# Taking node tiles by rank of edge count, and running each finished tile's norm, activation and next-layer tables between the gather's steps

## The reference, cut to what matters

```python
for l in range(4):
    h = einsum('ni,rio->rno', X, W[l])               # one table of rows for each of 4 relations
    msg = h[etype, src] * inv_deg[:, None]           # a row for each edge
    agg = segment_sum(msg, dst, num_segments=6250)
    out = agg + X @ root[l] + bias[l]
    out = layer_norm(out) * gamma[l] + beta[l]       # over the 256 features of a node
    X = elu(out) + X
```

## Time and profile before

| what | value |
|---|---|
| median of 3 runs | 8877.58 us (8870.69 to 8877.74) |
| the profiled execution's own time | 8865.25 us |
| its span in the trace | 8863.5 us |
| busy share of the span | PE 71%, PEld 40%, DVE 53%, ACT 15%, POOL 50% |
| granted TensorE clock, mean | 0.792 of full speed |

### The profile page before, as it was taken

One profiled execution on the slowest core, in us unless ns is written; L12 is line 12 of the kernel. 1 busy time (PEld: TensorE's weight loads), 2 busy tenths in 40 slices (PEclk: granted clock), 3 DMA queues, 4 the chain that ended last, 5 costly groups with the idle time before them and its releaser, 6 DMA issues. The chain is left out here.

```text
span 8863.5 us, 101707 instructions
## 1 busy us (share of the span) xinstructions
PE 6322.2 (71%) x18072; PEld 3511.4 (40%) x18072; DVE 4665.9 (53%) x14830; ACT 1360.0 (15%) x3463; POOL 4442.4 (50%) x4395
## 2 busy tenths in 40 slices
PE   0677777587777587777678998818849877774378
PEld 0343333244444244444334333305524444443355
DVE  6135555427777526777633555552243566662522
ACT  0221111231111131111031000002202111110122
POOL 0047777327777516777624777730000477773211
PEclk9988888797777697788687555559869888876789
DMA  2243333234444223333323333300014333330000
GB/s 66 77 136 105 105 105 105 67 106 117 117 117 117 76 91 113 111 112 111 95 73 105 105 105 105 105 24 0 0 45 140 121 105 105 105 105 19 0 24 16
DMA packets 424513, 765.22 MB, mean 86 GB/s; under 512 B 84857, under 2 KB 288845, under 8 KB 424194
## 3 DMA queue, kind: packets, MB, share of 16 engines
q0 software_dynamic: 200240, 547.36, 21.6%
q1 hardware_dynamic: 224206, 217.15, 7.2%
HBM read 587.30 MB, written 176.90 MB: 86 GB/s over the span
## 5 line engine op out<-in xcount | busy, mean ns | idle before, releaser
L477 POOL DMA_INDIRECT gnn_msg<-tables,gnn_row_ring x4160 | 3951.4, 950 | 2045.0 <-issue 1791.0
L521 PE MATMUL bank<-gnn_msg,gnn_hot 128*128 128x256 f32 x8320 | 3600.9, 541 | 1185.2 <-DMA gnn_msg<-tables,gnn_row_ring 701.1
L521 PEld LDWEIGHTS bank<-gnn_msg,gnn_hot 128*128 128x128 f32 x8320 | 1717.9, 248 | 2932.9 <-issue 1202.5
L507 DVE TENSOR_TENSOR sums<-sums,bank 128x256 f32 x4160 | 1745.2, 420 | 1613.6 <-PE bank L521 1489.9
L487 DVE TENSOR_SCALAR gnn_hot<-iota,gnn_meta_ring 128x128 f32<-128x128 f32 x3328 | 1139.0, 375 | 594.4 <-ACT gnn_meta_ring L469 594.4
L125 POOL TENSOR_TENSOR ve<-mv,eps 128x7 f32<-128x7 f32 x63 | 12.8, 203 | 1799.3 <-DVE mv L119 1651.7
L1017 PE MATMUL bank<-gnn_w,gnn_hot 128*128 128x512 f32 (+1 forms) x2352 | 905.0, 543 | 0.0
L468 ACT COPY gnn_row_ring<-row 128x8 int32 (+1 forms) x520 | 102.6, 197 | 3608.3 <-PE bank L521 3587.6
L1017 PEld LDWEIGHTS bank<-gnn_w,gnn_hot 128*128 128x128 f32 x2352 | 444.8, 196 | 446.2 <-issue 397.8
L1003 PE MATMUL bank<-ident,gnn_msg 128*128 128x128 f32 x392 | 66.0, 319 | 405.5 <-ACT gnn_msg L1062 243.5
L1581 PE MATMUL bank<-tables_w,sums 128*128 128x512 f32 x784 | 340.0, 595 | 6.4 <-ACTq L109 6.4
(11 more groups left out here) (371 smaller groups left out, 5692.4 us busy)
## 6 DMA issues: line engine op xcount, KB each, us to landing
tables<-gnn_msg SPq DMA_DIRECT2D x392, 256.0 KB, 2.1
gnn_msg<-tables,gnn_row_ring POOLq DMA_INDIRECT x4160, 2.7
tables<-sums SPq DMA_DIRECT2D x98, 512.0 KB, 2.9
first_norm<-state SPq DMA_DIRECT2D x1, 6272.0 KB, 27.9
gnn_w<-first_norm SPq DMA_DIRECT2D x49, 128.0 KB
mixer_rows<-gnn_ex SPq DMA_DIRECT2D x49, 128.0 KB, 1.8
gnn_w<-mixer_rows SPq DMA_DIRECT2D x49, 128.0 KB, 2.4
residual<-in_x_dram SPq DMA_DIRECT2D x1, 6144.0 KB
```

The lines of the kernel that those rows point to most:

```text
L477: self.nc.gpsimd.indirect_dma_start(out=self.msg[:, s, :], out_offset=None, in_=self.table, in_offset=bass.IndirectOffsetOnAxis(ap=self.ro ...
L507: self.nc.vector.tensor_tensor(at, at, self.c.bank[4 + s % 4][:, 0:D], ALU.add).then_inc(self.added, 1)
L521: self.nc.tensor.matmul(self.c.bank[4 + s % 4][:, 0:D], self.hot[:, s, :], self.msg[:, s, :], start=True, stop=True).then_inc(self.summed, 1)
```

## The change

- **Steps.** SLOTS becomes 17, and a layer has NT bodies of 17 steps (833). `edge_tables` ranks the tiles by edge count, smallest first, and lays the steps out by rank. The sum over all tiles fits in 49x17 steps, so after body i the tiles of the first i+1 ranks are complete.
- **Post.** A new class takes one tile in each body, the one that the body before completed (`ranked_tile` reads its number into a register of VectorE, ScalarE and SyncE). VectorE takes statistics at step 0, the inverse root at step 1, scale and shift at step 2; ScalarE takes Exp; VectorE finishes the activation at steps 6, 7 and makes the new state at step 8; TensorE turns it at step 10 and multiplies it by the next layer's weights at steps 12, 13 and 15; ScalarE evicts; SyncE stores two pieces of 256 KB. The next layer's tables go to a second table tensor, its root product into the tile's block of sums. In layer 3 only the part up to the new state is there.
- **Stages.** The tables stage stays for layer 0 alone. The norm stage is gone, with all that GpSimd did in it. A layer ends with a drain: `Post` and the job for the last tile, without gather steps.
- **Bias.** It becomes a matmul of a row of ones by the bias row, at the end of the root product, in the tables stage too.
- **Memory.** The input rows are stored to `x_d` at the start, and their SBUF space serves as scratch; Feed adds its result to rows loaded from there and stores them back; one load at the start of layer 3 brings them back. Keys0 loads its rows by DMA, where ScalarE copied them.
- **Inverse root** of one column: 9 dependent steps where there were 13. The wide one in the second graph layer takes 12.
- **Order.** ScalarE fills the ring for body i+1 in body i: the first half behind the job and Exp, the second behind the evictions. The jobs' two uses of banks 0 and 1 share bank 0; banks 1 and 3 serve `Post`. The second graph layer takes 49 bodies of 17 steps as well, and a drain.

```diff
-SLOTS = 16
+SLOTS = 17
+HALVES = ((0, 9), (9, 8))
+STEPS = NT * SLOTS
+SUM_SLOTS = 4
...
+                then(v.scalar_tensor_tensor(key[:], cnt[:], 64.0, no, ALU.mult, ALU.add))
+                then(v.tensor_tensor(pairs, over_inner(key[:]), over_outer(key[:]), ALU.is_le))
+                then(v.tensor_reduce(rank[:], pairs, AX.X, ALU.add))
+                then(v.tensor_tensor(pairs2, pairs, over_inner(nst[:]), ALU.mult))
+                then(v.tensor_reduce(incl[:], pairs2, AX.X, ALU.add))
+                then(v.tensor_tensor(excl[:], incl[:], nst[:], ALU.subtract))
+                then(v.tensor_scalar(over_all[:], rank[:], float(NT), float(1 << 20), ALU.is_equal, ALU.mult))
+                then(v.tensor_tensor(incl[:], incl[:], over_all[:], ALU.add))
+                then(v.tensor_tensor(pairs, over_inner(rank[:]), over_outer(c.iota[:, 1:NT + 1]), ALU.is_equal))
+                then(v.tensor_tensor(pairs2, pairs, over_inner(no), ALU.mult))
+                then(v.tensor_reduce(key[:], pairs2, AX.X, ALU.add))
+                then(v.tensor_copy(c.order[:], key[0:1, :]))
...
+                then(v.tensor_tensor(begun[:], begun[:], over[:], ALU.subtract))
+                for to, of in ((tile_f, no), (base_f, excl[:]), (s_f, start[:, 0:NT]), (end_f, start[:, 1:NT + 1])):
+                    then(v.tensor_tensor(prod[:], begun[:], wide(of), ALU.mult))
+                    then(v.tensor_reduce(to[:], prod[:], AX.X, ALU.add))
...
-        at = first + 4 + 3 * k
+        at = first + 3 + 2 * k
+        dve.wait_ge(s_step, at)
+        v.tensor_scalar(t, y, y, half, ALU.mult, ALU.mult).then_inc(s_step, 1)
+        dve.wait_ge(s_step, at + 1)
+        v.scalar_tensor_tensor(y, t, 1.5, y, ALU.add, ALU.mult).then_inc(s_step, 1)
+    dve.wait_ge(s_step, first + ROOT_STEPS)
...
+    def ring(self, act, i, n, h):
+        s0, w = HALVES[h]
+        act.wait_ge(self.summed, n * SLOTS + (s0 + w))
+        at = ds(i * SLOTS + s0, w)
+        self.nc.scalar.copy(self.row_ring[:, h, 0:w], self.rows[:, at]).then_inc(self.ring_ready, 1)
+        self.nc.scalar.copy(self.meta_ring[:, h, 0:w, :], self.c.meta[:, at, :]).then_inc(self.ring_ready, 1)
...
+            back = s - SUM_SLOTS + 1 if s >= SUM_SLOTS else max(k for k in range(SLOTS) if k % SUM_SLOTS == s) + 1 - SLOTS
...
+    def vector(self, dve, n, t, last=False):
+        v, c = self.nc.vector, self.c
+        agg, state = c.agg[:, ds(t * D, D)], c.xn[:, ds(t * D, D)]
+        def after(s):
+            if s == 0:
+                dve.wait_ge(c.edges.added, n * SLOTS + SLOTS)
+                v.bn_stats(self.bn, agg).then_inc(self.s_bn, 1)
+                dve.wait_ge(self.s_bn, n)
+                v.bn_aggr(self.mv, self.bn).then_inc(self.s_mv, 1)
+            if s == 1:
+                dve.wait_ge(self.s_mv, n)
+                inverse_root(dve, c, self.rs, self.half, self.tmp, self.mv[:, 1:2], self.s_root, n - 1)
+            if s == 2:
+                v.scalar_tensor_tensor(self.u, agg, self.mv[:, 0:1], self.vecs[:, 0, :], ALU.subtract, ALU.mult).then_inc(self.s_u1, 1)
+                dve.wait_ge(self.s_u1, n)
+                v.scalar_tensor_tensor(self.u, self.u, self.rs, self.vecs[:, 1, :], ALU.mult, ALU.add).then_inc(self.s_u2, 1)
+            if s == 6:
+                dve.wait_ge(self.s_exp, n)
+                v.tensor_scalar(self.ex, self.ex, 1.0, -1.0, ALU.min, ALU.add).then_inc(self.s_cut, 1)
+            if s == 7:
+                dve.wait_ge(self.s_cut, n)
+                v.scalar_tensor_tensor(self.u, self.u, 0.0, self.ex, ALU.max, ALU.add).then_inc(self.s_elu, 1)
+            if s == 8:
+                dve.wait_ge(self.s_elu, n)
+                if last:
+                    v.tensor_tensor(state, state, self.u, ALU.add).then_inc(self.s_new, 1)
+                else:
+                    dve.wait_ge(self.s_turned, n)
+                    dve.wait_ge(self.s_kept, n)
+                    v.tensor_tensor(self.xs, state, self.u, ALU.add).then_inc(self.s_new, 1)
+    def exponential(self, act, n):
+        act.wait_ge(self.s_u2, n)
+        self.nc.scalar.activation(self.ex, self.u, ACT.Exp).then_inc(self.s_exp, 1)
+    def tensor(self, pe, n):
+        c, t = self.c, self.nc.tensor
+        def after(s):
+            if s == 10:
+                pe.wait_ge(self.s_new, n)
+                pe.wait_ge(self.s_out, n * 3)
+                for h in range(KH):
+                    ins = t.transpose(c.bank[3][:, h * P:(h + 1) * P], self.xs[:, h * P:(h + 1) * P], c.ident[:])
+                ins.then_inc(self.s_turned, 1)
+            if s in (12, 13):
+                j = s - 12
+                if j == 0:
+                    pe.wait_ge(self.s_xt, n)
+                for h in range(KH):
+                    ins = t.matmul(c.bank[1 + 2 * j][:], self.xt[:, h, :], self.w[:, h, j * 512:(j + 1) * 512],
+                                   start=(h == 0), stop=(h == KH - 1))
+                ins.then_inc(self.s_prod, 1)
+            if s == 15:
+                pe.wait_ge(self.s_out, n * 3 + 1)
+                for h in range(KH):
+                    t.matmul(c.bank[1][:, 0:D], self.xt[:, h, :], self.w[:, h, REL0 * D:], start=(h == 0), stop=False)
+                t.matmul(c.bank[1][:, 0:D], c.ones[0:1, :], self.brow[:], start=False, stop=True).then_inc(self.s_prod, 1)
+    def scalar(self, act, n, t):
+        c, sc = self.c, self.nc.scalar
+        act.wait_ge(self.s_new, n)
+        sc.copy(c.xn[:, ds(t * D, D)], self.xs).then_inc(self.s_kept, 1)
+        act.wait_ge(self.s_turned, n + 1)
+        sc.copy(self.xt.rearrange("p h r -> p (h r)"), c.bank[3][:, 0:D]).then_inc(self.s_xt, 1)
+        for j in range(2):
+            act.wait_ge(self.s_store[j], n * 16)
+            act.wait_ge(self.s_prod, n * 3 + (j - 2))
+            sc.copy(self.outs[:, j, :], c.bank[1 + 2 * j][:]).then_inc(self.s_out, 1)
+        act.wait_ge(self.s_prod, n * 3)
+        sc.copy(c.agg[:, ds(t * D, D)], c.bank[1][:, 0:D]).then_inc(self.s_out, 1)
+    def sync(self, sp, n, t, table):
+        for j in range(2):
+            sp.wait_ge(self.s_out, n * 3 + (j + 1))
+            sp.dma_start(table.rearrange("(r n) d -> n r d", n=NP)[ds(t * P, P), 2 * j:2 * j + 2, :],
+                         self.outs[:, j, :].rearrange("p (r d) -> p r d", d=D)).then_inc(self.s_store[j], 16)
...
+                dve.wait_ge(self.s_first, i * 16)
+                dve.wait_ge(self.s_put, i * 16)
+                v.tensor_tensor(self.done, self.u, self.first_x, ALU.add).then_inc(self.s_done, 1)
...
+                            if j == 2:
+                                ins = nc.tensor.matmul(c.bank[b][:, 0:D], c.ones[0:1, :], brow[:], start=False, stop=True)
                             ins.then_inc(c.bank_full[b], 1)
...
+                    if l:
+                        sp.wait_ge(post.s_new, l * NT)
+                        vectors(l)
+                    work.begin_sync(sp, a)
+                    work.sync(sp, 0, True, False)
+                    with sp.Fori(1, NT) as i:
+                        work.sync(sp, i, True, True)
+                        post.sync(sp, i + l * NT, ranked_tile(sp, c, i - 1), c.tabs[(l + 1) % 2])
+                    work.sync(sp, NT, False, True)
+                    post.sync(sp, (l + 1) * NT, ranked_tile(sp, c, NT - 1), c.tabs[(l + 1) % 2])
+                    work.end_sync(sp)
...
+                for l, work in enumerate(behind):
+                    work.begin_tensor(pe)
+                    edges.tensor(pe, l * NT, work.tensor(pe, 0, True, False))
+                    pe.wait_ge(s_w, (l + 2) * 80)
+                    with pe.Fori(1, NT) as i:
+                        edges.tensor(pe, i + l * NT, both(post.tensor(pe, i + l * NT), work.tensor(pe, i, True, True)))
+                    drain(both(post.tensor(pe, (l + 1) * NT), work.tensor(pe, NT, False, True)))
+                    work.end_tensor(pe)
+                    pe.wait_ge(post.s_prod, (l + 1) * NT * 3)
                     pe.sem_inc(s_tabs, 1)
-                    if work:
...
+                    work.begin_scalar(act)
+                    work.scalar(act, 0, True, False)
+                    for h in range(2):
+                        edges.ring(act, 1, l * NT + 1, h)
+                    with act.Fori(1, NT) as i:
+                        n = i + l * NT
+                        t = ranked_tile(act, c, i - 1)
+                        work.scalar(act, i, True, True)
+                        post.exponential(act, n)
+                        edges.ring(act, i + 1, n + 1, 0)
+                        post.scalar(act, n, t)
+                        edges.ring(act, i + 1, n + 1, 1)
+                    t = ranked_tile(act, c, NT - 1)
...
+                    edges.vector(dve, 0, l * NT, work.vector(dve, 0, True, False))
+                    dve.wait_ge(s_vec, l * 32 + 32)
+                    with dve.Fori(1, NT) as i:
+                        n = i + l * NT
+                        t = ranked_tile(dve, c, i - 1)
```

(19 more changed lines are left out.)

596 lines of the change are left out of this document (278 added, 318 removed).

## The result

The changed kernel takes 8434.0 us in the median of three runs (8420.6 to 8445.9), the kernel before 8877.7 beside it (8870.7 to 8884.2); the ratio is 0.950, 95% interval 0.948 to 0.952. The change makes the kernel 444 us faster, a little under half of the 920 us that were forecast (7957 us), and the time lies above the range (7750 to 8230). One more run at a granted clock of 0.551 took 10044 us and stands outside the comparison, as does one of the kernel before beside the experiments (10230 us at 0.563). The profiled execution took 8445.9 us, its span is 8444.1.

The account below looks back on a forecast made before the run. GpSimd's indirect-DMA issue bounds the gathers, with VectorE becoming the bound in layers 1 and 2. Terms -1176 + 198 + 16 + 18 + 22 + 3 = -919 gave 7957 us, range 7750 to 8230.

Parts of the forecast that it names:

- the stages removed: Between gathers and after gather 3: 1250.7 us without fetches go, drains sum to 75 us in their place, -1176 us.
- The layers' beginnings: Layers 1 and 2: late parameter loads leave VectorE and TensorE standing some 8 us each, +16 us (0 to 20).
- VectorE in a body: Gathers in layers 1 and 2: VectorE needs 22.7 us a body, above GpSimd's 21.3, and becomes the bound.
- How well the queues mesh: Layers 1 and 2: 0.5 us a body for waits between engines, between 0 and 2.7, giving 23.2 us.
- poor meshing: Rival: a fixed place waits each body; 25.5 us in layers 1 and 2, 22.5 in layer 0; 8230 us; chance 0.19.
- Table loads hidden: ScalarE with Feed: two function-table loads of 1.28 us each body, hidden; 98 loads expected.
- Bias matmul: Tables stage, bound by TensorE: two records of 256 columns a tile, +22 us (0 to 25).
- Second graph layer: Second graph layer: one step and a drain more, +3 us.
- Fetched loop bodies: Rival: longer VectorE loop bodies are fetched anew each turn, 225 us in layers 1 and 2; 8180 us; chance 0.08.
- The clock: Rival: new bodies granted a clock of 0.54, TensorE needs 27 us a body in three layers; 8600 us; chance 0.05.
- All hidden: Rival: VectorE's waits overlap the new work and 21.3 us a body holds in all layers; 7760 us; chance 0.15.
- The slower case: Rival: each body waits for its tile's whole chain, 36 us a body in three layers; 9920 us; chance 0.03.

Follow-up runs that it names:

- The aligned kernel: The changed kernel with a body's tile numbers 20 words apart, so each half's register load begins at a multiple of 4 words: 8191.7 us, ratio 0.9224.
- the later places: TensorE's turning, wide products and root product one step later, against the kernel with aligned tile numbers and cheaper root: 8109.2 us, ratio 0.9142.
- the split block: Job's moments and root moved from behind its rows to later separate steps, against the kernel with aligned tile numbers and cheaper root: 8102.2 us, ratio 0.9136.
- the aligned kernel with the cheaper root: Aligned tile numbers plus scalar_tensor_tensor as first operation of each root round: 8149.1 us, ratio 0.9182; with Gelu also replaced by Relu, 8153.3 us, ratio 0.9194.
- The combined kernel: Changed kernel plus aligned numbers, cheaper root, split root, TensorE's turning place later behind layer 0 alone, and early save of input rows: 8028.4 us, ratio 0.9038.

## Why the prediction was wrong

**What bounds the kernel, and the stages removed.** Right: the 1250.7 us went. The drains cost more than their 64 us (3 x 21.3): the three gaps came to 99.5. In them VectorE's last addition ends 12 to 18 us after the last issue, where 4.6 were taken, since it lags behind GpSimd's issues; from there to the next gather's first issue it is 17 to 18 us, near the 15.5 of the chain. The layers' beginnings, put at 8 us each, lie not in the gaps but inside gathers 1 and 2: their first product starts 13.9 and 10.6 us after the first issue, against 2.9 in gather 0, so this term was right. The last layer's chain took 11 as forecast (5512.3 to the state's last addition at 5522.9).

**VectorE in a body: the step that failed.** "One more register read +0.3" was right for one number more (the load of the ranked tile's number takes 0.31 us in the trace), and the two bulk reads stayed in the base of 17.5 at 0.6 each. Nothing in the sum asked where a read begins. With 17 steps and halves of 9 and 8 it begins off a multiple of 4 words three times in four, and the two bulk reads need 3.4 us a body instead of 1.2, or of 1.45 when aligned. The aligned kernel prices it at 242 us, half of the miss; in the traces 238 us of it stand in gathers 1 and 2. With it the bodies there left the range's upper end of 25.5 us. The row that would have warned is the 0.60 us at the body's edge ("issue ... 0.6"): I read it as a fixed price.

**The root.** The job's root was to save 0.8 us and the post's to take 1.8. The new first operation with two scalars from memory takes 0.27 us where the old ones took 0.16, so from its first step to the operation behind it the root of 9 steps lasts 2.19 us (2614.27 to 2616.46), against 2.48 for 13 (4007.63 to 4010.11): the job's saves 0.3. Changing its form gave 43 us back.

**How well the queues mesh.** 0.5 us a body was taken, with 2.7 as the upper end. In the aligned kernel VectorE waits 2.8 us a body for TensorE in gathers 1 and 2, the upper end, though it needs only some 21.4 (24.2 less 2.8) and not 22.7; the two errors cancel in part, and the bodies last 24.4 and 23.9 against 23.2. Of these waits 16.9 and 21.9 us are the single one at each gather's start, which the forecast had as another term; without them it is 2.5 and 2.3 a body. In layer 0, held to be under GpSimd's pace, TensorE's fixed places were worth 48 us: here "poor meshing" was right (22.5 a body; it is 22.9 aligned). Moving the places shows that they were the cause, and the trace points to the one at step 10. What the remaining 2.3 to 2.5 us in gathers 1 and 2 are made of stays open: neither the later places nor the split block took them away.

**ScalarE, SyncE, GpSimd.** Table loads hidden: right, shown on the aligned kernel with the cheaper root. There are 145 of them in Feed, not 98, since a copy reloads too (L1033). The row load at step 1 costs TensorE little at the given places; it becomes a wait when the products move back.

**Edge preparation** +17 us of +18: right, 2.66 us a pass. **Bias matmul** +42 for +22: two records of 256 columns were put at 0.43 us a tile by their columns, and take 0.69 (34.0 us for 49 tiles); the rest goes with the longer other products, at a granted clock of 0.91 against 0.99 before, for which the forecast had put 1 us. The saves of input rows, not in the sum, cost 16. Together with the edge preparation that is 35 of the +42 of the start; 7 stay open.

**Second graph layer** +17 us for +3. 8 are its last drain (13.0 us from the last issue to the end of VectorE's last copy of the stage, against 5.2), since with 49 bodies for 49 tiles the last tile's job stands in the last body. The other 9 are the last stage of the kernel, with the same operations at another granted clock, 0.94 before and 0.91 after. Three other traces with the same code there have it some 7 us shorter, at 0.93, so most of the 9 us need not be the change's (windows of that stage, before, then after):

```profile
8434.00:8863.00 429.00, 355.49 (x1330) 246.35 (x1330) 85.06 (x193) 113.88 (x161) 67.42 (x28) 0.94 0.07 21
```

```profile
8005.00:8443.00 438.00, 364.11 (x1330) 251.10 (x1330) 85.09 (x193) 114.55 (x161) 67.47 (x28) 0.91 0.06 21
```

**The rivals.** Fetched loop bodies: refuted, the instruction queues moved 44 packets against 46 before. The clock: refuted for the gathers, 0 and 2 were granted 0.94 and 0.92 and 3 0.66, against 0.87, 0.82 and 0.59 before; it fell in the tables stage and perhaps at the end, as told above. All hidden: refuted, 26.4 and 26.8 us a body are not 21.3. The slower case, 36 us a body, did not come either. Poor meshing was right for gather 0 and, as the waits of the aligned kernel show, for its 2.8 us a body in gathers 1 and 2; but half of the miss had a cause that no rival named, and both together pass the 8230 that it was given.

**The account of the 477 us** between forecast and median: register reads 242, the root's form 43, TensorE's places in layer 0 48, saves 16, bias 20 above its term. Together 369. Of the rest, some 17 stand in the second graph layer and 9 in gather 3. In the trace of the kernel with aligned reads and the cheaper root, gathers 1 and 2 are still 43 and 25 us over their forecast, beginnings included. The 47 us of the split block are a saving and no term that was missed: the block and its waits were there before and lay in the base of 17.5. The combined kernel, which has all but the bias repaired, ends 71 above the forecast, and its trace 85 above the 7944: 26 at the start, 3, 28, -8 and 14 in gathers 0 to 3, 6 in the gaps, 1 before the second graph layer and 14 from there to the end.

## What to carry to other kernels

When a size changes (here 16 to 17 steps), go through everything that indexes with it, the small register loads too, and ask for each where it begins: an address that was aligned by luck has a price in no row of before. Queue time that the profile does not count as busy belongs in an engine's sum as soon as that engine is near the bound; the same fault cost 22 us in one kernel and 242 in the other. And a wait in an in-order queue is best priced by moving its place by one step: in gather 0 48 of 75 us came back, and in gather 2 another wait took its place.

## What the runs showed of the hardware

A register load of 8 numbers on VectorE takes 0.60 us when its first word is at a multiple of 4 words and 1.85 when not; one of 9 takes 0.84 and 2.07. It was seen for first words that leave 1, 2 and 3 on division by 4, in 490 and 520 loads a run. The Trainium skill ("Runtime: NRT & Kernel Launch", Instruction fetch mechanics) gives some 200 ns for each register even in bulk. These loads come from SBUF; the unaligned ones are near that with 0.23 us a register, and the aligned ones, at 0.075 a register for eight, differ from it, so here the measurement holds. An operation of VectorE on 128x1 with two scalars from memory took 0.273 us, with one scalar and a tensor 0.222, against 0.16 for a tensor_tensor of the same size.
